# Attention and mixture-of-experts block on one core: the attention part's instruction orders written anew for all five engines

## What is computed

```python
mod = silu(c) @ wmod                       # six vectors of 128 per sample
h = layernorm(x) * (1 + ca) + sa
q, k, v = split(rms_norm(h) @ w_qkv.T)     # each rms_norm'ed but v
w = exp(k)
y = sigmoid(q) * cumsum(w * v) / (cumsum(w) + 1e-6)
u, g = split(y @ w_swiglu.T)
x = x + ga * (h + (u * silu(g)) @ w_out.T)
h = layernorm(x) * (1 + cb) + sb
# top-1 router over 16 experts, capacity 320; rank of a token = how many
# tokens of all earlier positions chose the same expert
out = x + gb * prob * expert(gelu(h @ w1[e]) @ w2[e])
```

## Time and profile before

| | |
|---|---|
| median of 3 runs | 231.9 us |
| profiled execution, its own time | 229.94 us |
| span of the profiled execution | 227.7 us |
| mean granted TensorE clock | 0.951 |
| busy: TensorE, VectorE, ScalarE, GpSimd | 86%, 66%, 64%, 52% |

### The profile page before, as it was taken

The page is one execution under the profiler, slowest core; times in us unless marked ns, Lnnn a source line. Parts: engine busy times, 40 slices in busy tenths (PEclk is TensorE's granted clock), DMA queues, the critical chain, the costliest instruction groups (busy, mean ns, idle before and its releaser), DMA issues.

```text
span 227.7 us, 4034 instructions
## 1 busy us (share of the span) xinstructions
PE 196.4 (86%) x1177; PEld 157.9 (69%) x1177; DVE 151.1 (66%) x472; ACT 145.5 (64%) x425; POOL 117.3 (52%) x143
## 2 busy tenths in 40 slices
PE   7995999999999999859867487999999999999151
PEld 4885587797888787647653234887887888889141
DVE  2669679999989989968863408074765856662121
ACT  4396679999999789857544721686586685824000
POOL 6317443131888284748557460000785577577733
PEclk9999799999998899999999679999999999999957
DMA  5999999239340051142343216999969724410100
GB/s 154 290 350 360 359 331 354 77 88 286 95 169 16 3 188 46 38 150 101 113 159 119 83 36 136 366 358 358 341 203 308 250 78 143 138 40 27 35 23 13
DMA packets 37284, 38.60 MB, mean 170 GB/s; under 512 B 2591, under 2 KB 31334, under 8 KB 37264
## 3 DMA queue, kind: packets, MB, share of 16 engines
q1 hardware_dynamic: 33936, 31.29, 43.4%
q0 software_dynamic: 3328, 7.07, 8.7%
HBM read 19.19 MB, written 18.95 MB: 167 GB/s over the span
## 4 chain that ended last, share of the span: by engine, by line
PE 56%; DVE 18%; issue 7%; another core or an unknown queue 7%; POOL 5%; ACT 3%; DMA 2%; POOLq 1%; DVEq 0%; SPq 0%; ACTq 0%
PE bank L1280 13%; PE bank L1266 12%; PE bank L1039 4%; PE bank L1057 3%; PE bank L1050 3%; PE bank L1029 2%; PE bank L1083 2%; PE bank L1190 2%; PE bank L1078 2%; PE bank L1109 2%; POOL xh L294 2%; DVE kvsum L780 2%; DVE w1l L955 2%; PE bank L1244 2%
## 5 line engine op out<-in xcount | busy, mean ns | idle before, releaser
L529 POOL DMA_INDIRECT out_dram<-x_all,rest x40 | 44.1, 1101 | 45.5 <-issue 41.4
L503 POOL DMA_INDIRECT dispatched_rows<-rows,slot x32 | 32.2, 1006 | 18.9 <-issue 9.3
L709 ACT ACTIVATE HT<-bank 128x320 f32<-128x320 f32 x64 | 28.0, 438 | 18.2 <-remote 9.1
L1280 PE MATMUL bank<-HT,w 128*128 128x320 f32 x112 | 32.4, 432 | 0.0
L1280 PEld LDWEIGHTS bank<-HT,w 128*128 128x128 f32 x112 | 20.6, 189 | 6.7
L1266 PE MATMUL bank<-xth,w1h 128*128 128x320 f32 x64 | 22.6, 353 | 0.3 <-DVE xtl L961 0.3
L977 DVE SCALAR_TENSOR_TENSOR junk<-bank,rest 128x128 f32<-128x128 f32 x40 | 11.5, 344 | 14.6 <-remote 10.3
L955 DVE TENSOR_TENSOR w1l<-w,w1h 128x1024 fp32r<-128x1024 f32 x8 | 16.1, 2026 | 6.9 <-DMA dispatched_rows<-rows,slot 6.9
L1266 PE MATMUL bank<-xth,w1l 128*128 128x320 f32 x64 | 19.8, 309 | 0.0
L1266 PE MATMUL bank<-xtl,w1h 128*128 128x320 f32 x64 | 19.8, 309 | 0.0
L1004 DVE COPY OT<-bank 128x320 f32<-128x320 f32 x14 | 6.9, 492 | 18.4 <-PE bank L1280 17.4
(11 more groups left out here) (172 smaller groups left out, 503.3 us busy)
## 6 DMA issues: line engine op xcount, KB each, us to landing
w<-in_L_ffn_w_dram SPq DMA_DIRECT2D x16, 512.0 KB, 9.7
dispatched_rows<-blank SPq DMA_DIRECT2D x8, 965.0 KB, 12.2
rest<-dispatched_rows SPq DMA_DIRECT2D x8, 645.0 KB
hin<-dispatched_rows SPq DMA_DIRECT2D x7, 320.0 KB, 10.9
x_all<-in_L_attn_x_dram SPq DMA_DIRECT2D x8, 256.0 KB, 6.1
rows<-gb_row SPq DMA_DIRECT2D x8, 256.0 KB, 3.7
out_dram<-rows SPq DMA_DIRECT2D x8, 256.0 KB
out_dram<-x_all,rest POOLq DMA_INDIRECT x40
```

What stands on the lines that cost most here:

```text
L503: pool.indirect_dma_start(out=disp_d, out_offset=bass.IndirectOffsetOnAxis(ap=slot[:, b, j:j + 1], axis=0), in_=rows[:, b, j, :], in_offse ...
L529: pool.indirect_dma_start(out=out_d.rearrange("b t d -> (b t) d"), out_offset=bass.IndirectOffsetOnAxis(ap=rest[i % RING][:, n, C_TOK - D: ...
L709: act.activation(HT[e][:, f, :], ps_h[c % HB][:, 0:CAP], ACT.Gelu_apprx_tanh).then_inc(h_done, 1)
L1280: last = pe.matmul(ps_o[e], w2[i % RING][:, e, f, :], HT[e][:, f, :], start=(f == 0), stop=(f == NF - 1))
```

## The change

The bodies of all steps are as before, except that each list of steps in the attention part is written in another order, and that some movable steps are called on another engine:

| step | engine before | engine now |
|---|---|---|
| normalize1 | VectorE 0, 3; GpSimd the rest | VectorE 0, 1, 2; GpSimd the rest |
| modulate1 | VectorE 2, 4, 5; ScalarE 0, 1, 3, 6, 7 | VectorE 0, 2 to 5; ScalarE 1, 6, 7 |
| weigh_sums | VectorE 1, 2; GpSimd the rest | VectorE 2, 4; GpSimd the rest |
| silu | VectorE 1, 4, 6, 7; GpSimd 0, 2, 3, 5 | VectorE 1, 3, 5, 6, 7; GpSimd 0, 2, 4 |
| normalize2 | VectorE 0; GpSimd 3; ScalarE the rest | VectorE 0; GpSimd 1, 2, 4; ScalarE 3, 5, 6, 7 |
| modulate2 | VectorE 1, 6; ScalarE the rest | ScalarE all |
| h2_rows | ScalarE all | VectorE 2; ScalarE the rest |

Two of the unread products near the start (`run_early(2)`) are gone, and those near the end are placed and sized anew. The expert part is untouched. Two lines of the GpSimd list, before and now:

```diff
-            weigh_sums(pool, 4); squares(7); count_seen(1); scatter(1); weigh_sums(pool, 5)
+            normalize2(pool, 2); count_seen(0); scatter(0); count_seen(1); scatter(1); silu(pool, 4)
```

More of the change, by code:

```diff
@@ L657, in _ @@
[L657 to L673, removed]
+            ln1_scale(0); keep_weights(); keep_more(); ln1_scale(1); square_sums(0); ln1_scale(2); rms_scales(0)
@@ L931, in _ @@
[L931 to L948, removed]
@@ new lines, in _ @@
+            weigh_v(3); normalize2(dve, 0); silu(dve, 1); modulate1(dve, 5); denominator(3); gate_u(1)
+            qk_means(4); weigh_sums(dve, 2); scan_kv(3); weigh_v(4); residual(1); clamp_g(2)
+            stats2(1); h_means(5); aggregate2(1); scan_w(4); shift2(1); scan_kv(4); aggregate1(7)
+            qk_means(5); denominator(4); gate_u(2); shift1(7); weigh_v(5); residual(2); scan_w(5)
+            clamp_g(3); scan_kv(5); denominator(5); h_means(6); stats2(2); top_value(0); aggregate2(2)
@@ L1198, in _ @@
[L1198 to L1209, removed]
@@ L1210, in _ @@
[L1210 to L1215 removed]
+            transpose1(0); weights_over(); run_early(1); project_qk(0); h_square_sums(0); transpose1(1)
@@ new lines, in _ @@
+            row_product(2); transpose_k(3); project_v(3); project_qk(4); project_v(4); transpose_kv(3)
+            transpose_q(3); project_u(1); transpose1(6); project_out(1); transpose_k(4); project_g(2)
+            h_square_sums(5); transpose_kv(4); project_qk(5); project_v(5); row_product(3)
+            transpose_q(4); project_u(2); transpose2(0); project_out(2); transpose_k(5)
+            transpose_kv(5); project_g(3); h_square_sums(6); transpose1(7); transpose_q(5); logits(0)
+            h2_back(0); transpose2(1); project_v(6); project_qk(6); ranks(0); logits(1); h2_back(1)
@@ new lines, in _ @@
+            project_u(3); transpose2(2); project_g(4); ranks(1); project_out(3); logits(2)
+            h_square_sums(7); project_qk(7); ranks(2); transpose_k(6); project_v(7); transpose_q(6)
+            transpose_kv(6); project_u(4); h2_back(2); transpose_k(7); project_g(5); project_out(4)
+            transpose_kv(7); transpose_q(7); transpose2(3); project_u(5); run_late(128); logits(3)
+            h2_back(3); project_out(5); project_g(6); ranks(3); project_u(6); run_late(256)
+            transpose2(4); run_late(256); project_g(7); logits(4); project_out(6); ranks(4)
```

83 lines of the change are left out of this document (56 added, 27 removed).

## The result

The changed kernel took **235.65 us** (median of 4 runs, 234.69 to 238.62), the kernel before 231.97 us (4 runs). The ratio is 1.023, with a 95% interval of 1.017 to 1.030: slower by about 5 us (disturbed runs are left out of the ratio, so it isn't that of the two medians), where 226.0 was forecast and 232.5 was the upper end of the range. The profiled execution took 234.89 us with a span of 232.6 and a mean granted clock of 0.932 (before 229.94, 227.7 and 0.951). Of the 4.9 us by which the span grew, 3.9 lie ahead of the experts (w1l at 141.04, before 137.13) and 1.0 in the expert part, which the change didn't touch (91.6 us, before 90.6).

A forecast was written before the change was run, and what follows sets the result against it. Attention full to about 90 us, then a drain set by waits around GpSimd's scatters. Residual(7) 1.5 us earlier plus 3.2 us cut behind it gave 4.7: 229.94 to 225.2, moved to 226.0 us for the median; range 220.5 to 232.5.

The forecast's parts named there:

- the walk: Attention part: new step lists followed at traced durations without friction; residual(7) 3.2 us earlier, scatter 3 at 99.7, 3.6 earlier.
- GpSimd then has scatters 0 and 1 back to back, 73.3 to about 84: GpSimd near 80 us: silu(4), weigh_sums(5) and so project_g(5) wait behind both scatters; project_g(5) at about 86.5 to 87.
- the frictions: Unknown wait and low-clock spells that the walk omits; 1.7 us taken back, leaving residual(7) 1.5 us earlier, at 112.6.
- The drain: Last samples, after some 100 us: no engine full, 5.1 us of GpSimd's scatter intervals are waits, source of most gain.
- The 3.2 us "that go": From residual(7) to slots of sample 7: 1.66, 0.7 and 0.84 us of waits removed, 16.1 us becoming 12.9.
- The early lag: Start of sample 0's output half: silu(0) at about 38, gate_u(0) at about 39.1, 6.1 us later than before.
- the output half catches up: Attention part: project_out(2) starts near 60.8 in both orders, residual(3) at 77.5 to 79 against 78.53 before.
- The lag that is never made up: Rival: output half and every scatter stay 6.1 us late, 236.0 us; decided by residual(3) after about 83; chance 0.16.
- The rival of clock and scatters: Rival: low clock in two TensorE places costs 5.2 us, 1.7 already counted; about 228.7 us; chance 0.27.
- that sign of being wrong: Between 65 and 90 us: the clock at 0.5 for more than 3 us would show the forecast wrong.
- Its first place: TensorE's 3.6 us from h_square_sums(6) to transpose2(1): clock falls; project_v(6) and project_qk(6) take 0.9 and 1.7 us longer.
- An edit that cost nothing: GpSimd's normalize1(5) meets both diagonals on VectorE, losing 1.9 us, covered as the sample is needed some 20 us later.

The follow-up runs named there:

- 1, old, pair: Kernel before with one edit: on GpSimd scatter 0 issued right ahead of scatter 1, eight indirect DMAs in a row; 236.25 us, ratio 1.022.
- 4, old, first: Kernel before without scatters 0 and 1, first run, on another chip than its partner; 229.08 us, ratio 0.983.
- 4, old, second: Kernel before without scatters 0 and 1, run again side by side with the changed kernel without them; 228.68 us, ratio 0.998.
- 6, old: Kernel before without the indirect DMAs that send the rows of expert pairs 5 and 6 to the output; 223.52 us, ratio 0.967.
- 7, old: Kernel before without GpSimd's two drains behind its sends of expert pairs 1 and 3; 227.75 us, ratio 0.995.
- 5, after again: Changed kernel as it is, repeated beside the one with scatters set apart; 236.38 us, ratio 1.018.
- 2, new: Changed kernel with silu(4) between scatter 0 and scatter 1 on GpSimd; 235.62 us, ratio 1.016.
- 3, new, no rows: Changed kernel with all row indices of scatters 0 and 1 out of bounds, same DMAs moving no rows; 235.91 us, ratio 1.026.
- 5, new, apart: Changed kernel with GpSimd's scatters 0, 1 and 2 set apart by other steps; 233.98 us, ratio 1.012.
- 7, new, apart: Changed kernel with its three first scatters set apart and without the two drains among the sends; 232.24 us, ratio 1.013.
- 4, new, first: Changed kernel without scatters 0 and 1, first run; 232.49 us, ratio 0.993.
- 4, new, second: Changed kernel without scatters 0 and 1, run again side by side with the kernel before without them; 228.79 us, ratio 0.998.
- experiment 8: No new kernel or time: fourteen traces read together for the 55 waits of 0.5 us or more without a known releaser ahead of the experts.

## Why the prediction was wrong

**The landmarks of all executions.** Start times in us; the last column is the time from `residual(5)` to the slots of sample 7. The executions "1, old, pair" and "4, old, first" were the longest of their kernels' runs.

| kernel | residual(0) | residual(3) | residual(5) | slots(7) | w1l | span | 5 to slots |
|---|---|---|---|---|---|---|---|
| before | 35.94 | 78.53 | 99.76 | 130.10 | 137.13 | 227.7 | 30.3 |
| 1, old, pair | 37.51 | 79.36 | 105.47 | 136.00 | 143.50 | 236.8 | 30.5 |
| 4, old, first | 37.37 | 79.24 | 98.96 | 129.37 | 136.77 | 229.1 | 30.4 |
| 4, old, second | 34.36 | 76.19 | 95.06 | 125.60 | 133.08 | 224.5 | 30.5 |
| 6, old | 37.31 | 82.49 | 103.71 | 132.34 | 139.39 | 221.0 | 28.6 |
| 7, old | 34.69 | 77.14 | 98.46 | 129.05 | 136.32 | 225.1 | 30.6 |
| after | 43.05 | 83.22 | 103.73 | 133.99 | 141.04 | 232.6 | 30.3 |
| 5, after again | 45.03 | 85.17 | 105.25 | 135.32 | 142.78 | 234.6 | 30.1 |
| 2, new | 45.36 | 82.66 | 104.98 | 134.83 | 142.24 | 233.2 | 29.9 |
| 3, new, no rows | 43.64 | 83.83 | 104.33 | 134.10 | 141.55 | 232.8 | 29.8 |
| 5, new, apart | 43.56 | 80.86 | 99.41 | 128.65 | 136.07 | 229.8 | 29.2 |
| 7, new, apart | 46.76 | 83.96 | 102.54 | 131.57 | 139.04 | 228.7 | 29.0 |
| 4, new, first | 43.25 | 79.31 | 97.20 | 127.36 | 134.77 | 228.5 | 30.2 |
| 4, new, second | 43.06 | 79.12 | 97.05 | 129.04 | 136.09 | 226.7 | 32.0 |

**The step that failed** is in the walk: "GpSimd then has scatters 0 and 1 back to back, 73.3 to about 84", costed by what is queued behind them on GpSimd alone, while the row that spoke of the real price, the 1.96 us "of unknown cause" at `residual(5)`, was put among the frictions and taken back with 1.7 us in all. That wait had a cause that could have been found: it ends next to a scatter of four DMAs. I asked what waits for GpSimd, and not what else happens while it issues. The place was right (scatter 0 started at 74.44, scatter 1's last DMA ended at 84.8); the price was missing. `project_g(5)`, put at 86.5 to 87 by what is queued on GpSimd, came at 94.39. From `residual(0)` to the slots of sample 7, so that the differing starts drop out, the new order takes 90.3 to 90.9 us with the pair (three executions) and 84.8 and 85.1 with the scatters apart; the old one 98.5 with the pair and 94.2 to 95.0 without it. **The pair costs about 5.6 us in the one and 4 in the other**, the latter from a single trace, that of the longest run of its kernel.

**The drain, wrongly improved.** The forecast took `residual(7)` 14.4 us behind `residual(5)`, as before, and cut the 16.1 us behind it to 12.9. After: 18.0 and 12.3. The cut came out as predicted, and the stretch ahead of it grew by as much. A part is plain: `residual(7)` now stands behind `slots(5)` in VectorE's list (121.49, then 121.70) and starts 1.4 us after the record of its product ends (120.33). But the old order did the same in other executions: in three of its six `residual(7)` came 17.7 to 18.0 us behind `residual(5)` and the slots 12.6 or 12.7 behind that, where the profiled execution before had 14.4 and 16.0. The last column says it at a glance: 28.6 to 30.6 us in the old order, 29.0 to 32.0 in the new. The 3.2 us "that go" from behind the residual were slack that can as well lie ahead of it. One reason lies in the three waits of experiment 8: 4.4 us of late reads stand behind the very waits of GpSimd (1.74 and 1.71 ahead of scatters 4 and 5, 2.89 ahead of scatter 7) from which "most of a gain must come". Such reads come with the scatters, so that an earlier result need not remove them. The changed kernel has one again ahead of its scatter 4:

```profile
114.81 0.59 ACT L349 COPY rows<-bank 128x512 f32<-128x512 f32 x1 [1.80 <-remote]
```

That this is what keeps the drain at 29 to 32 us in both orders is argued from these rows; no kernel without scatters 3 to 6 was run. This term was 3.2 of the 4.7 us forecast; the case without the two scatters comes nearest to what was left of the forecast when the first error is taken away: no gain over the old order, where the prediction had 2%.

**The early lag.** `gate_u(0)` was put at 39.1 and came at 39.86; `residual(2)` at 64.08 stood only 1.3 us behind the 62.78 of before. So "the output half catches up" was right, and without the two scatters it held on (`residual(3)` at 79.12 and 79.31).

**The rivals.** The lag that is never made up gave 236.0 us and its test, `residual(3)` after 83, was met (83.22). It came within 0.4 us of the measured median by luck: the lag had been made up but for 1.3 us by 64 us, and the scatters brought a new one. The rival of clock and scatters named the right place, "TensorE has almost nothing for 3 us", but put it down to the late `weigh_sums(5)` and a clock that would cost 3.5 us. The clock did fall there (0.50 from 86 to 90 us), so that sign of being wrong was met as well, but behind the late reads. Its first place fell out: in the run of transposes and narrow products, 65.6 to 69.4 us, the clock stayed at 1.00, and so it did up to 84 us:

```profile
66.00:68.00 2.00, 2.00 (x21) 2.00 (x20) 2.00 (x3) 1.43 (x3) 0.00 (x0) 1.00 0.98 283
```

The Trainium skill, "TensorE: Matmul & The Clock Gate", part on the transpose through TensorE, by which this stretch had to lose the clock, isn't borne out here; the measurement decides.

**An edit that cost nothing, and sometimes did.** GpSimd's `normalize1(5)` took 3.69 us as predicted. But the cover was read for its own result only. `squares(3)` stands behind it on GpSimd, and TensorE waits for that:

```profile
28.80 3.69 POOL L294 TENSOR_SCALAR xh<-x_all,rs,nm 128x128 f32<-128x128 f32 x4 [1.50 <-DVE nm L738]
```

```profile
33.55 1.05 PE L1028 MATMUL bank<-tri,hsq 128*128 128x1 f32 x8 [1.85 <-POOL hsq L485]
```

In the changed kernel's profiled execution the clock held. In three of the eight executions with the new order it fell within 3 us behind this hole, here in the last kernel of experiment 7:

```profile
32.00:34.00 2.00, 0.15 (x2) 0.05 (x1) 2.00 (x7) 1.80 (x7) 1.89 (x3) 1.00 1.08 284
34.00:36.00 2.00, 2.00 (x9) 1.85 (x10) 0.47 (x8) 2.00 (x8) 0.00 (x0) 0.58 1.07 274
36.00:38.00 2.00, 2.00 (x6) 1.01 (x5) 1.54 (x6) 0.47 (x1) 1.04 (x1) 0.50 1.03 368
```

Those are the three with `residual(0)` at 45.03, 45.36 and 46.76 in the table; the other five have it at 43.05 to 43.64. That this fall comes from the hole is argued, not shown: no kernel without the hole was run. In one of the five, the first of experiment 4, the clock fell ahead of it (0.50 from 26 to 28 us), and `residual(0)` was no later for it (43.25).

**What stays open.** The pair explains what the stretch near 80 us lost, but not the whole slowdown. With the scatters apart the new order starts the experts 1.1 us before the old one in the profiled execution, and it is still 1.2% slower than the kernel before by its ratio, and 1.8% slower than the old order where both lack the drains. The fall at 34 us, in some executions only, would explain 2 to 3.7 us of it where it occurs. Another part may be the expert part: with the same instructions it took 90.6 us in the kernel before and 93.7 with the scatters apart, where ScalarE's last unknown wait was 9.61 us in place of 8.17. But the old order with the pair took 93.3 us for it, so this need not come from the order. Nor is it known what in the issue of an indirect DMA holds up TensorE's results.

## What to carry to other kernels

Look at every wait with an unknown releaser and ask what the *other* engines were doing; here each one of 0.5 us or more ahead of the experts came in or just behind GpSimd's issue of indirect DMAs, and an order that puts two such issues back to back can make a result wait for both. A gain measured from one landmark to the end is only worth what the distance between two fixed landmarks loses: compare that distance over several executions, since a step that comes early just waits further on. And when an edit is covered by "its result isn't needed yet", read also what stands behind it on its engine.

## What the runs showed of the hardware

While GpSimd issues indirect DMAs, what TensorE has finished by its record can be read late, by VectorE, ScalarE and GpSimd alike. Beside a scatter of four the waits reached 2.1 us (1.96 at 99.76, 2.05 and 2.06 in experiments 1 and 6), and in 48 of 55 cases the reader started 5.5 to 6.3 us behind the scatter's start. Beside a row of eight, results were read 3.8 to 6.6 us behind the end of their records, and at the end of a row of 16 sends 7.9 us behind it. Not every result in such a row is late (0.8 us at 79.36 in experiment 1; next to nothing at 205.94 in the kernel before). The waits of the row of eight stay when its DMAs move no rows.

TensorE itself works on in the meantime with what it has (79.58 to 82.4 in the changed kernel), and results of another engine aren't held up in this way: in experiment 1, inside the row, `sg` was ready on ScalarE at 83.05 and VectorE's reader started at 83.27, while the transposes that ended at 83.44 were read at 87.36. The scatters' DMAs took 0.97 to 1.35 us each in all traces, so nothing in GpSimd's own rows tells of it.
